# Head products of an mLSTM block in f16 halves with pairs summed on VectorE, and the next sequence's statistics moved behind the last chunk's heads

## Chip, cores and metric

One NeuronCore of a Trainium2 chip runs the whole program; the other cores are idle. The metric is the device time of one execution in microseconds. The kernel before took 1876.2 us, the median of 3 runs (1874.89 to 1881.56).

## The reference

Sixteen sequences of 512 tokens with 512 features pass through one block: layer norm, an mLSTM attention with 8 heads (query and key width 32, value width 64), a per-head norm, an output gate and a projection, all added to x; then layer norm and a feed-forward part of 2048 units whose weights are made ternary.

```python
def step(carry, xs):                       # over the 512 tokens of a sequence
    f_log = jax.nn.log_sigmoid(f_t)
    m_new = jnp.maximum(f_log + m, i_t)
    F = jnp.exp(f_log + m - m_new)
    I = jnp.exp(i_t - m_new)
    C_new = F[..., None, None] * C + (I[..., None] * k_t)[..., :, None] * v_t[..., None, :]
    n_new = F[..., None] * n + I[..., None] * k_t
    qs = q_t * scale
    h_num = jnp.einsum('bhd,bhdv->bhv', qs, C_new)
    qn = jnp.einsum('bhd,bhd->bh', qs, n_new)
    denom = jnp.maximum(jnp.abs(qn), jnp.exp(-m_new)) + EPS
    h = h_num / denom[..., None]
...
h_norm = _multihead_norm(h, gamma)         # (h - mean) * rsqrt(var + EPS) * gamma, per head
y = (jax.nn.sigmoid(o_preact) * h_norm) @ Wout.T
x = x + y                                  # layer norm of x goes in
x = x + gelu(layernorm(x) @ w1_q.T + b1) @ w2_q.T + b2
```

## The kernel before

The recurrence is computed in its chunked form. A sequence is four chunks `j` (or token tiles `t`) of 128 tokens. For each head the scores of a chunk (keys by queries, from f16 halves) are multiplied with a decay factor into the tile `dec` (f32, keys on the partitions) and masked; `vaug` holds the values of a tile with a column of ones appended, 8 heads x 65 columns. The product of `dec` and `vaug` gives numerator and normaliser of a head, and the state of the earlier chunks (`cst`) is added by a second product with the weighted queries `qw`.

Every engine's program is written out by hand, in order, and the engines meet by semaphores alone. The order of TensorE is that of `sequence(b, fb, ahead)`: the attention of sequence `b` interleaved with the feed-forward part of sequence `fb = b - 1`. In its order: `gates` (L1567), values (`tokens`, `late_values`), keys and queries (`features`), output gate; `up` of 16 feed-forward tiles (`hidden`), with the scores between them; then `down` in sixteen quarters. Four of these quarters carry a head chunk: `chunk(j, t, q)` calls `down` with `j`, and after each of its 8 matmuls comes one `chunk_head` (L1684), an f32 product of 128x128 weights (`dec`) and 65 columns (`vaug`) into one of the four banks of `psh`; the profile shows it as two records. At the end of a sequence `project` (L1692) multiplies the transposed, gated heads (`hoT`) with the output weights, tile by tile, with quarters of `down` between the first three of them; projections 2 and 3 follow each other, then come the gates and the values of the next sequence. Sequence 0 has no feed-forward part beside it; there the heads stand alone, and the weights of the feed-forward part are prepared between them. Behind the last attention there is only the feed-forward part of sequence 15.

PSUM banks alternate: `pa` by the number of its use, so the gates take the bank that `residual` of tile 2 frees, and the values the bank that `residual` of tile 3 frees. `psh` is one set of banks for all four chunks: chunk j+1 waits for `ph_free`, which VectorE gives when it has read chunk j.

The chain of a chunk's heads, from `ph_fill` on: VectorE `head_stats` (L1248): denominators `den` and sums `hsum` from `psh`, centred heads `cent` (in `kT`) from `psh`, which frees it; ACT `squares` (L868); VectorE reduces these to `hvar`; POOL `head_norm` (L572): a power (L574) and a multiplication (L577); VectorE `gated` (L1284), which for chunk j stands inside `head_stats` of chunk j+1 and for chunk 3 by itself; ACT `gated_hi` (L872) and POOL `gated_lo` (L579) make f16 halves; SP issues the transposing DMA into `hoT` (L487).

VectorE's order behind the heads matters here: `head_stats` of a chunk, `result` (`done`, L1333) of a feed-forward tile, `next_stats` (the layer norm statistics of `x` of sequence b+2, which sits in `xin`, L1106), then `gated(b, 3)`, `residual` (L1293) of tiles 0 and 1, `norm_apply` (L1120) of sequence b+2, and `residual` of tiles 2 and 3 with the last `result` between them. POOL beside it adds the bias to the residual (`residual_bias`, L584) and computes 1/sqrt (`layer_norm`). ACT's `tokens_hi` of the next sequence waits for `norm_apply`.

## Time and profile before

| | |
|---|---|
| median of 3 runs | 1876.2 us |
| profiled execution | 1875.94 us, span 1874.2 us |
| TensorE matmul busy | 1811.6 us, 97% |
| TensorE weight load busy | 945.5 us, 50% |
| VectorE busy | 1178.1 us, 63% |
| ACT busy | 1034.3 us, 55% |
| POOL busy | 507.4 us, 27% |
| TensorE clock granted | 0.98 of 2.4 GHz over the span, full in the middle |

Read the busy times with care: matmuls overlap in the records, so a share of 97% means a stream without holes rather than 97% of the array's peak. The page's other two parts that matter are its chain of the work that ended last and its costliest groups. For the rest the timeline of one sequence is read, that of sequence 9 with the window from 987 to 1034 us; its pattern repeats in sequences 1 to 13. In a timeline a row is a start, a duration, and what ran; "x2" are two records that follow each other.

### The profile page before, as it was taken

What the parts mean: (1) busy time and instruction counts of PE and PEld (TensorE: products, weight loads), DVE (VectorE), ACT (ScalarE), POOL (GpSimd) and SP (SyncE); (2) the same over time, 40 slices, a digit from 0 to 9 for tenths busy, and PEclk for the clock granted to TensorE, in tenths of its full rate; (3) what the DMA queues carried; (4) which work ended last, traced back from release to release, by engine and by line L of the source; (5) the groups of instructions that cost most, each with busy time, mean ns of one, the idle gap of its engine ahead of it and who ended that gap; (6) DMA issues with size and microseconds to landing.
All of it is one profiled execution on the core that took longest, in us unless ns stands there. A gap on an engine that the chain in (4) does not pass through costs nothing.

```text
span 1874.2 us, 30222 instructions
## 1 busy us (share of the span) xinstructions
PE 1811.6 (97%) x11900; PEld 945.5 (50%) x11900; DVE 1178.1 (63%) x2259; ACT 1034.3 (55%) x1711; POOL 507.4 (27%) x394
## 2 busy tenths in 40 slices
PE   5769999999999999999999999999999999999989
PEld 3454554545455454545545454554545445454544
DVE  6686575665757566575765657576565756645542
ACT  5757647274563727456372745737274473736523
POOL 1342131412314141231413123141312214131220
PEclk8879999999999999999999999999999999999989
DMA  8434125240422515042251503225150332413010
GB/s 278 145 102 119 29 61 129 51 139 24 129 39 52 139 46 144 23 117 51 52 138 46 145 23 106 62 51 139 46 144 17 103 72 51 117 45 99 12 40 23
DMA packets 233517, 156.86 MB, mean 84 GB/s; under 512 B 195088, under 2 KB 199312, under 8 KB 228256
## 3 DMA queue, kind: packets, MB, share of 16 engines
q1 hardware_dynamic: 231792, 151.79, 30.8%
q10 hardware_dynamic: 1584, 3.15, 0.5%
q8 instruction: 94, 1.54, 0.3%
q14 instruction: 47, 0.39, 0.1%
HBM read 90.48 MB, written 17.24 MB: 57 GB/s over the span
## 4 chain that ended last, share of the span: by engine, by line
PE 92%; DVE 2%; ACT 1%; issue 1%; DMA 0%; POOL 0%; POOLq 0%; DVEq 0%; ACTq 0%
PE pf L1714 24%; PE pf L1728 24%; PE pa L1606 19%; PE pa L1582 8%; PE psh L1606 6%; PE psh L1687 5%; PE psh L1681 1%; PE psh L1665 1%; PE pa L1573 1%; PE psh L1647 1%; PE psh L1620 1%; ACT dec L842 0%; DVE x2T L1078 0%; DVE dec L1245 0%; DVE x2T L1090 0%
## 5 line engine op out<-in xcount | busy, mean ns | idle before, releaser
L1728 PE MATMUL pf<-w2T,gT 128*128 128x512 f16 x2048 | 535.8, 379 | 0.0
L1714 PE MATMUL pf<-x2T,w1T 128*128 128x512 f16 x2048 | 457.2, 381 | 0.8 <-DVE x2T L1322 0.6
L1330 DVE SCALAR_TENSOR_TENSOR gT<-g,wscale,gT 128x512 f16<-128x512 f32 x256 | 214.7, 839 | 287.2 <-ACT gT L865 287.2
L1728 PEld LDWEIGHTS pf<-w2T,gT 128*128 128x128 f16 x2048 | 223.9, 111 | 175.9
L1714 PEld LDWEIGHTS pf<-x2T,w1T 128*128 128x128 f16 x2048 | 194.1, 98 | 234.3 <-issue 2.5
L862 ACT ACTIVATE g<-pf,b1c 128x512 f32<-128x512 f32 x256 | 175.6, 686 | 100.9 <-PE pf L1714 88.5
L1606 PE MATMUL pa<-wT,xT 128*128 128x512 f16 x960 | 213.6, 380 | 1.0 <-ACT sig L801 0.9
L870 ACT ACTIVATE ktok<-kT 128x512 f32<-128x512 f32 x64 | 40.3, 630 | 315.0 <-DVE kT L1268 315.0
L1687 PEld LDWEIGHTS psh<-vaug,dec 128*128 128x128 f32 x1024 | 183.0, 193 | 15.4 <-DVE cst L1234 1.2
L865 ACT ACTIVATE gT<-g,wscale 128x512 f16<-128x512 f32 x256 | 184.8, 722 | 8.4
L574 POOL TENSOR_TENSOR hinv<-hvar,half 128x8 f32<-128x8 f32 x64 | 105.0, 1640 | 298.4 <-DVE hvar L1281 298.4
L1606 PE MATMUL pa<-wT,hoT 128*128 128x512 f16 x768 | 177.3, 385 | 3.8 <-DVE xT L1131 3.8
L1582 PE MATMUL pa<-xT,wT 128*128 128x512 f16 x768 | 171.4, 379 | 0.1
L1687 PE MATMUL psh<-vaug,dec 128*128 128x65 f32 x1024 | 168.9, 252 | 0.9 <-DVE cst L1234 0.9
L842 ACT ACTIVATE dec<-dec,gtok 128x128 f32<-128x128 f32 x512 | 154.2, 390 | 0.0
L561 POOL TENSOR_SCALAR_AFFINE_SELECT dec<-dec 128x1024 f32<-128x1024 f32 x64 | 76.8, 1201 | 280.4 <-DVE dec L1245 280.4
L1606 PEld LDWEIGHTS pa<-wT,xT 128*128 128x128 f16 x960 | 92.6, 98 | 114.0 <-issue 7.0
L570 POOL TENSOR_TENSOR qw<-qw,qT 128x768 f32<-128x768 f32 x16 | 56.6, 3537 | 335.1 <-ACT sig L801 175.1
L581 POOL TENSOR_TENSOR qT<-kT,qT 128x512 f16<-128x512 f32 x64 | 74.3, 1161 | 198.1 <-ACT qT L877 198.1
L1606 PE MATMUL psh<-wT,xT 128*128 128x512 f16 x576 | 126.9, 379 | 0.0
L1606 PEld LDWEIGHTS pa<-wT,hoT 128*128 128x128 f16 x768 | 75.7, 99 | 96.0 <-issue 8.0
L1582 PEld LDWEIGHTS pa<-xT,wT 128*128 128x128 f16 x768 | 74.4, 98 | 87.1 <-DVE wT L1053 0.4
(202 smaller groups left out, 2154.9 us busy)
## 6 DMA issues: line engine op xcount, KB each, us to landing
dec<-gate_r SPq DMA_DIRECT2D x32, 1024.0 KB, 6.5
xin<-L_attn_x SPq DMA_DIRECT2D x16, 1024.0 KB, 5.3
out<-x1b SPq DMA_DIRECT2D x64, 256.0 KB, 2.2
xres<-L_attn_x SPq DMA_DIRECT2D x16, 512.0 KB, 6.3
xres<-L_attn_x SPq DMA_DIRECT2D x32, 256.0 KB, 2.9
qw<-gate_w SPq DMA_DIRECT2D x128, 48.0 KB, 5.8
gT<-L_ffn_w SPq DMA_DIRECT2D x5, 1024.0 KB, 5.0
gT<-L_ffn_w ACTq DMA_DIRECT2D x3, 1024.0 KB, 6.3
```

Of the source, the lines that this page charges most:

```text
L561: nc.gpsimd.affine_select(out=rows_of, in_=rows_of, compare_op=ALU.is_ge, fill=0.0, base=0, pattern=[[0, 2 * T], [1, P]], channel_multipli ...
L574: nc.gpsimd.tensor_tensor(hinv[:, :], hvar[:, :], half[:, :], ALU.pow).then_inc(pool_a, 1)
L581: nc.gpsimd.tensor_tensor(head_parts[j % 2][:, LO, :], cent[j % 2], head_parts[j % 2][:, HI, :], ALU.subtract).then_inc(ho_lo[j], 1)
L842: last = nc.scalar.activation(dec[:, h, tok(j)], dec[:, h, tok(j)], ACT.Exp, bias=gtok[:, j, ROW_C, h:h + 1])
L862: nc.scalar.activation(g32[:, f % 2, :], pf[:, use % 2, :], ACT.Gelu, bias=b1c[:, f:f + 1], scale=1.0 / X_SCALE).then_inc(pf_free[use % 2], 1)
L865: nc.scalar.activation(gT[:, HI, f, :], g32[:, f % 2, :], ACT.Copy, scale=wscale[:, W_GELU:W_GELU + 1]).then_inc(g_hi, 1)
L1330: nc.vector.scalar_tensor_tensor(gT[:, LO, f, :], g32[:, f % 2, :], wscale[:, W_GELU:W_GELU + 1], gT[:, HI, f, :], ALU.mult, ALU.subtract) ...
L1582: last = nc.tensor.matmul(bank, wT[:, ws, k, col:col + P], xT[:, xs, :, k, :], start=(k == 0 and n == 0), stop=(k == KD - 1 and n == 2))
L1606: last = nc.tensor.matmul(bank, src[:, xs, k, :], wT[:, ws, k, col:col + D], start=(k == 0 and n == 0), stop=(k == KD - 1 and n == 2))
L1687: last = nc.tensor.matmul(psh[:, i, g * VA:(g + 1) * VA], dec[:, h, tok(j)], vaug[:, j, h, :], start=(j == 0 and g == 0), stop=(g == HG - ...
L1714: last = nc.tensor.matmul(bank, w1T[:, k, tok(f)], x2T[:, part, :, k, :], start=(k == 0 and part == HI), stop=(k == KD - 1 and part == LO))
L1728: last = nc.tensor.matmul(bank, gT[:, part, f, tok(t)], w2T[:, f, :], start=(f == 0 and part == HI), stop=(f == NF - 1 and part == LO), sk ...
```

## The change

In all sequences but number 0 a head product becomes two f16 products. The decay tile and the values are each split in a high and a low half (high: the value rounded to f16; low: the rest), the two value halves of a head lie side by side (130 columns), and both decay halves are multiplied with this pair. PSUM then holds two columns for each result, and VectorE adds them in one reduction over the pair (`head_sum`, in SBUF), which also frees `psh`. In sequence 0 the product stays f32 and VectorE copies the result to `head_sum`. Scales are moved so that the halves fit in f16.

The splits are new operations: high halves of the values by POOL (`value_hi`, 4), low halves by VectorE (`value_lo`, 4); high halves of the decay by ACT (`decay_hi`, 4), low halves by VectorE for chunks 0 and 1 and by POOL for 2 and 3 (`decay_lo`). The high and low halves of chunk j overwrite the f32 decay of chunk j-1, those of chunk 0 lie in `qT`. So each `decay_hi` waits for the `decay_lo` before it. The value halves share their memory with `hoT` and with the halves of keys and queries.

The statistics of the next x (`next_stats`) no longer stand between the chunks' `head_stats`: tiles 0 and 1 come behind the last `head_stats`, tiles 2 and 3 behind `residual` of tile 0. In sequence 0 all four come there.

```diff
+        shared = sb("shared", [P, T * NH * 2 * VA], F16)
+        hoT = shared[:, 0:T * 2 * D].rearrange("p (t a k c) -> p t a k c", t=T, a=2, k=KD)
+        vparts = shared[:, :].rearrange("p (t n w) -> p t n w", t=T, n=NH)
...
-        by_bank = psh[:, :, 0:HG * VA].rearrange("p h (a v) -> p a h v", v=VA)
-        heads, norms = by_bank[:, :, :, 0:DHV], by_bank[:, :, :, DHV]
+        by_bank = psh[:, :, 0:HG * 2 * VA].rearrange("p h (a w v) -> p a h v w", a=HG, w=2)
+        sum_by_group = head_sum.rearrange("p (a h) v -> p a h v", a=HG)
+        heads, norms = sum_by_group[:, :, :, 0:DHV], sum_by_group[:, :, :, DHV]
...
+            def value_hi(b, t):
+                pool.wait_ge(pa_fill, pa_filled(b, score_use(NH - 1)))
+                nc.gpsimd.tensor_copy(vparts[:, t, :, 0:VA], vaug[:, t, :, :]).then_inc(vhi_ok, 1)
+
+            def decay_lo(b, j):
+                pool.wait_ge(dec_hi_ok, at(b - 1, T, j + 1))
+                nc.gpsimd.tensor_tensor(dec_parts(j)[:, :, LO, :], dec[:, :, tok(j)], dec_parts(j)[:, :, HI, :],
+                                        ALU.subtract).then_inc(dec_lo_ok[j], 1)
...
                     earlier_only(b, n)
+                    if n in (1, 2) and not first:
+                        value_hi(b, 2 * n - 2)
+                        value_hi(b, 2 * n - 1)
+                if not first:
+                    decay_lo(b, 2)
                 head_norm(b, 0)
+                if not first:
+                    decay_lo(b, 3)
...
+            def decay_hi(b, j):
+                if j == 0:
+                    act.wait_ge(masked, at(b, NH // 2, NH // 2))
+                    act.wait_ge(qw_ok, at(b, 1, 1))
+                    act.wait_ge(kq_split, at(b, 2, 2))
+                else:
+                    act.wait_ge(dec_lo_ok[j - 1], at(b - 1, 1, 1))
+                nc.scalar.activation(dec_parts(j)[:, :, HI, :], dec[:, :, tok(j)], ACT.Copy).then_inc(dec_hi_ok, 1)
...
-                    for f in range(NF):
+                    for f in range(NF - 3):
                         gelu(fb, f)
+                    decay_hi(b, 0)
+                    for f in range(NF - 3, NF):
+                        gelu(fb, f)
+                    decay_hi(b, 1)
...
+                if run_f:
+                    decay_hi(b, 2)
                 squares(b, 0)
                 if run_f:
                     sigmoids(b)
+                    decay_hi(b, 3)
...
+            def value_lo(b, t):
+                dve.wait_ge(vhi_ok, at(b - 1, T, t + 1))
+                nc.vector.tensor_tensor(vparts[:, t, :, VA:2 * VA], vaug[:, t, :, :], vparts[:, t, :, 0:VA],
+                                        ALU.subtract).then_inc(vlo_ok, 1)
...
-                nc.vector.tensor_tensor(den_of, norms, gtok[:, j, ROW_EM, :].rearrange("p (a h) -> p a h", h=H4), ALU.max)
+                if isinstance(b, int) and b == 0:
+                    nc.vector.tensor_copy(sum_by_group, by_bank[:, :, :, :, 0]).then_inc(ph_free, 1)
+                else:
+                    nc.vector.tensor_reduce(sum_by_group, by_bank, AX.X, ALU.add).then_inc(ph_free, 1)
+                dve.wait_ge(ph_free, at(b, PH_USES, U_H + j + 1))
+                nc.vector.scalar_tensor_tensor(den_of, gtok[:, j, ROW_EM, :].rearrange("p (a h) -> p a h", h=H4),
+                                               head_scale[:, 0:1], norms, ALU.mult, ALU.max)
...
                 state(b, 1)
-                hidden(10, 11, 12)
-                between(0)
-                state(b, 2)
-                hidden(13, 14, 15)
+                for t in range(T):
+                    if run_f:
+                        value_lo(b, t)
+                    hidden(10 + t)
+                    if t == 2:
+                        between(0)
+                        state(b, 2)
+                if run_f:
+                    decay_lo(b, 0)
+                    hidden(14, 15)
+                    decay_lo(b, 1)
...
                 head_stats(b, 0, ca)
                 done(0)
-                if run_f:
-                    next_stats(0)
...
                 done(2)
-                next_stats(*(range(3, T) if run_f else range(T)))
+                if run_f:
+                    next_stats(0, 1)
                 gated(b, 3)
                 between(4)
                 between(5)
                 residual(b, 0, ca)
+                next_stats(*(range(2, T) if run_f else range(T)))
...
             def chunk_head(b, j, h):
...
+                    parts = dec_parts(j)
+                    nc.tensor.matmul(psh[:, i, 2 * g * VA:2 * (g + 1) * VA], parts[:, h, HI, :], vparts[:, j, h, :],
+                                     start=(j == 0 and g == 0), stop=False, skip_group_check=True)
+                    last = nc.tensor.matmul(psh[:, i, 2 * g * VA:2 * (g + 1) * VA], parts[:, h, LO, :], vparts[:, j, h, :],
+                                            start=False, stop=(g == HG - 1), skip_group_check=True)
```

## Rows read from the trace of the kernel before

**Rows 1.** The page: the chain that ended last, by engine.

```profile
PE 92%; DVE 2%; ACT 1%; issue 1%; DMA 0%; POOL 0%; POOLq 0%; DVEq 0%; ACTq 0%
```

**Rows 2.** Timeline of TensorE, sequence 9 (start us, duration us, engine, line, what).

```profile
989.37 0.38 PE L1728 MATMUL pf<-w2T,gT 128*128 128x512 f16 x1
...
991.67 3.62 PE L1728 MATMUL pf<-w2T,gT 128*128 128x512 f16 x16
...
1023.75 3.62 PE L1728 MATMUL pf<-w2T,gT 128*128 128x512 f16 x16
1027.20 5.34 PE L1606 MATMUL pa<-wT,hoT 128*128 128x512 f16 x24
1032.47 1.49 PE L1573 MATMUL pa<-xT,wgT 128*64 128x512 f16 x12
1033.89 2.76 PE L1606 MATMUL pa<-wT,xT 128*128 128x512 f16 x12
```

**Rows 3.** Timeline of VectorE (DVE), the same sequence.

```profile
991.94 0.17 DVE L1259 TENSOR_TENSOR den<-psh,gtok 128x8 f32<-128x8 f32 x1 [2.64 <-PE psh L1687]
...
1013.68 0.17 DVE L1259 TENSOR_TENSOR den<-psh,gtok 128x8 f32<-128x8 f32 x1 [2.39 <-PE psh L1687]
1013.77 0.68 DVE L1260 TENSOR_REDUCE hsum<-psh 128x8 f32<-128x512 f32 x1
...
1017.08 0.17 DVE L1281 SCALAR_TENSOR_TENSOR hvar<-hsum,den 128x8 f32<-128x8 f32 x1
...
1021.10 0.69 DVE L1290 SCALAR_TENSOR_TENSOR kT<-kT,sig 128x512 f32<-128x512 f32 x1 [1.68 <-POOL kT L577]
1021.70 0.75 DVE L1300 SCALAR_TENSOR_TENSOR xres<-pa,evac,xres 128x512 f32<-128x512 f32 x1
1022.49 0.69 DVE L1303 BATCH_NORM_STATS2 stats<-xres 128x6 f32<-128x512 f32 x1
...
1025.99 2.78 DVE L1123 TENSOR_SCALAR xin<-xin,mean,rstd 128x512 f32<-128x512 f32 x4 [0.49 <-POOL rstd L541]
...
1032.58 0.75 DVE L1300 SCALAR_TENSOR_TENSOR xres<-pa,evac,xres 128x512 f32<-128x512 f32 x1 [0.32 <-PE pa L1606]
```

**Rows 4.** Timeline of ACT: the cast of the last gelu.

```profile
987.79 0.72 ACT L865 ACTIVATE gT<-g,wscale 128x512 f16<-128x512 f32 x1
```

**Rows 5.** DMA issues of the sequence (median us from issue to landing).

```profile
hoT<-qT SPq DMA_TRANSPOSE x4, 3.2
```

**Rows 6.** Timeline of TensorE, sequence 0: first and last of twelve in a row.

```profile
112.97 0.22 PE L1526 MATMUL pf<-ident,x2T 128*128 128x128 f16 x1
...
113.58 0.22 PE L1528 MATMUL pf<-ident,x2T 128*128 128x128 f16 x1
```

**Rows 7.** Groups by line, shapes apart (busy us, mean ns of one).

```profile
L1143 DVE SCALAR_TENSOR_TENSOR gT<-xres,gT 128x1024 f16<-128x1024 f32 x30 | 36.5, 1215 | 4.3 <-ACT gT L741 4.3
...
L741 ACT ACTIVATE gT<-xres 128x1024 f16<-128x1024 f32 x30 | 31.6, 1052 | 0.4
...
L1714 PEld LDWEIGHTS pf<-x2T,w1T 128*128 128x128 f16 x2048 | 194.1, 98 | 234.3 <-issue 2.5 <-DVE x2T L1322 1.0 <-ACT g L862 0.7
```

**Rows 8.** Timeline of POOL, sequence 9, chunk 3.

```profile
1018.31 1.63 POOL L574 TENSOR_TENSOR hinv<-hvar,half 128x8 f32<-128x8 f32 x1
...
1022.53 1.16 POOL L581 TENSOR_TENSOR qT<-kT,qT 128x512 f16<-128x512 f32 x1 [1.46 <-ACT qT L877]
1023.64 1.27 POOL L590 TENSOR_TENSOR x1b<-xres,b2r 128x512 f32<-128x512 f32 x1
```

**Rows 9.** Timelines of POOL and VectorE, sequence 0, where both work.

```profile
113.64 1.04 POOL L577 TENSOR_TENSOR kT<-kT,hinv 128x512 f32<-128x512 f32 x1
...
114.04 0.17 DVE L1263 SCALAR_TENSOR_TENSOR den<-psh,den 128x8 f32<-128x8 f32 x1
114.12 0.58 DVE L1264 TENSOR_SCALAR hsum<-hsum 128x8 f32<-128x8 f32 x1
```

**Rows 10.** Timeline of TensorE, sequence 0: a wait for the weight preparation.

```profile
147.95 0.27 PE L1526 MATMUL pf<-ident,x2T 128*128 128x128 f16 x1 [2.16 <-DVE x2T L1092]
```

More of the change, by code:

```diff
@@ L38 @@
 TOP = 2.0 ** 15
+V_SPLIT = 2.0 ** -5 / X_SCALE
+SCORE_SPLIT = 2.0 ** -16
 TINY = 2.0 ** -100
@@ L254, in block_program @@
         kq_split = sem("kq_split")
+        vhi_ok, vlo_ok = sem("vhi_ok"), sem("vlo_ok")
+        dec_hi_ok = sem("dec_hi_ok")
+        dec_lo_ok = [sem(f"dec_lo_ok{j}") for j in range(T)]
+        cent_ok = sem("cent_ok")
         sq_ok = sem("sq_ok")
@@ L1419, in sequence @@
                 done(1)
-                if run_f:
-                    next_stats(2)
                 weights_out(*USES_OUT[2:4])
@@ L1674, in chunk_state @@
                     pe.wait_ge(masked, at(b, NH // 2, NH // 2))
+                    if not (isinstance(b, int) and b == 0):
+                        pe.wait_ge(vlo_ok, at(b - 1, T, T))
+                if not (isinstance(b, int) and b == 0):
+                    pe.wait_ge(dec_lo_ok[j], at(b - 1, 1, 1))
                 if j == 1:
```

61 lines of the change are left out of this document (37 added, 24 removed).

## Prediction

> **What bounds the kernel now.** I read the page's chain of the work that ended last first [rows 1]: 92% of it is TensorE, so the end moves only by what TensorE's own stream gains, less the idle time that a late partner puts into it. Next comes TensorE's timeline in one middle sequence [rows 2]. The reader should see the pattern in a chunk: one matmul of `down` (128x512), then the two records of one f32 head product, then the next `down` matmul 0.38 us after the last. Then VectorE's timeline in the same sequence [rows 3], for when it comes to each head chunk and to each projection; then ACT, SP and POOL beside it [rows 4, 5, 8].
>
> **TensorE's part.** A pair of one `down` matmul and one head lasts 0.383 us (989.37 to 991.67 holds six), a `down` matmul alone 0.216 (1023.75 to 1027.20 holds sixteen) [rows 2]. So a head costs 0.383 - 0.216 = 0.167 us. The streamed columns don't change: f32 went twice over 65, f16 goes twice over 130. What changes are the weight loads. The nearest price of the new form is the run of twelve f16 128x128 matmuls, each with its own load: 0.61 us for eleven starts, 0.0555 us each at full clock [rows 6]. With 130 columns that is 0.0564, two are 0.113, and a head saves 0.054; since both f16 loads of a pair stand beside short matmuls I take 0.051. The bounds are a loss of 0.029 (each f16 product costs the 0.098 that its load lasts) [rows 7] and a gain of 0.054. Heads that change: 32 in each of 15 sequences, 480. **Gain: 480 x 0.051 = 24.5 us** (bounds -14 and 26), and a chunk's pitch falls from 7.25 (three pitches between 991.94 and 1013.68) [rows 3] to 6.84 us.
>
> The Trainium skill ("TensorE: Matmul & The Clock Gate", Back-to-back issue gap) gives about 81 ns for each matmul of 128 columns in a stream of loads and matmuls. By it the two would cost 0.162 and the gain would be 3 us. The trace's own run of such pairs disagrees [rows 6], and I go by the trace.
>
> **What is added elsewhere, up to chunk 0.** POOL gets four casts (128x520) behind the second and third mask; POOL is idle between masks and nobody waits before 988.8, so nothing. ACT gets four 128x1024 casts of 1.05 us, as L741 [rows 7]. The first stands ahead of gelu 13 of 16, where ACT has some 0.75 us spare, and delays it by about 0.3 us; TensorE needs that bank 0.9 us later. The second follows the last gelu. VectorE gets four `value_lo` of 128x520, 0.69 us, and two `decay_lo` of 1.21 us, as L1143 [rows 7]: 5.2 us in all. It idles about 1 us between two `gelu_lo` there, so this fits too; `decay_lo(0)` ends near 987.3 and TensorE wants it at 988.6. If that cover is gone, each us costs 15.
>
> **What is added to the head chain.** Let t = 0 be the moment when VectorE sees chunk 0 finished. After `gelu` 15 (its cast starts at 987.79) [rows 4] come decay_hi(1), decay_lo(1), decay_hi(2): 988.5 + 1.05 + 1.25 + 1.05 = 991.95, and t = 0 is 991.94 - 8 x 0.051 = 991.53. So POOL's `decay_lo(2)` starts at t = 0.5. Its price: POOL's f16 subtract of 512 elements takes 1.16 us, L581 [rows 8], so about 2.25 for 1024.
>
> `head_stats` grows: a reduce of 1040 elements from PSUM. That of 512 takes 0.68 [rows 3]; of this some 0.14 is fixed, as L1143 shows with 1024 in 1.21 [rows 7], and the rest goes by elements: 0.14 + 1040 / 512 x 0.54 = 1.23. The low bound is a second 0.68 (output is only 520), the high one 2.3 (if a reduction over pairs goes at half rate). From its start to `hvar` it took 3.40 us (1013.68 to 1017.08) and will take 4.66.
>
> And its small operations change place. `norms` and `heads` were in PSUM and are now in SBUF beside another SBUF operand. What that means the trace shows where POOL works at the same time: L1263, which reads PSUM, took its 0.17 us at 114.04 in the middle of POOL's L577, and L1264 behind it, which works within SBUF and takes 0.16 as a rule, took 0.58 and ended with it, 114.70 against 114.68 [rows 9]. So an operation of VectorE within SBUF that comes second waits for POOL's to end, and I take the same for the new forms of `den` and `cent`, and for POOL behind VectorE.
>
> The Trainium skill ("SBUF — State Buffer", Who interferes with whom) says it as an exclusive lock that a VectorE instruction with two SBUF inputs contends for, and one with a single SBUF input outside the two-port modes does not. It speaks against this change, which turns PSUM inputs into SBUF ones; were the lock only for L1264's kind, rival 1 would be the outcome.
>
> Walked through, in t:
> - Stats 0: reduce to 1.3, then `den` is held by POOL's decay_lo(2) to 2.75; hvar 6.6, result(0) to 7.3. It starts chunk 1 at 7.3, not 6.84.
> - POOL: pow 1.63 and multiply 1.04 [rows 8, 9] to 9.6, then decay_lo(3) (ACT has its high half about then, behind the sigmoid) from 9.7 to 12.0. Stats 1 stand still for it: `cent` at 12.2 to 12.5, hvar at 14.3, chunk 2 begun at 14.4 where 13.7 was possible.
> - Stats 2 end at 20.0, result(1) 20.7; stats 3 begin at 20.7 (possible: 20.5), lose 1 us to POOL's multiply of chunk 2, hvar 26.3. POOL's gated_lo(2), pow and multiply follow: gated(3) starts at g = 30.4 (30.4 to 30.85 by who comes first at 8.6). Before, it was 1021.10 - 991.94 = 29.16 [rows 3], with TensorE 1.24 us slower. Without the two POOL holds I get g = 29.2.
>
> **Behind the heads, where it is due.** TensorE ends the second-last projection (12 matmuls from 1027.20) 16.1 us after chunk 3's heads, starts the gates at 18.8 and the values at 20.2 (1013.68 against 1029.8, 1032.47, 1033.89) [rows 2, 3], which is now t = 36.6, 39.3, 40.7. It needs bank 0 from residual(2) at 39.3 and bank 1 from residual(3) at 40.7. VectorE's queue between: gated 0.61, residual 0.78, bn_stats 0.69, the moved next_stats(2,3), like bn_stats, 1.32, and mean_var, seven small operations, some 0.85, held 0.5 by POOL's residual_bias(0), L590, 1.27 us [rows 8]; residual(1) 0.78, bn_stats 0.69; norm_apply, which waits for POOL's rstd and residual_bias(1) and then takes 1.65 (1025.99, 2.78 with the wait for L590 in it) [rows 3]; then residual(2), bn_stats, result(3), residual(3): 2.9. That is g + 11.55: residual(3) is done at 41.95, not 40.7. In the profile before it is done at 1033.33 against 1033.89, 0.5 us ahead [rows 2, 3]. **Stall: 1.3 us per sequence** (0.1 with g = 29.2, 1.7 with 30.85), in the 13 sequences that still have a next x to normalise (1 to 13): -16.9 us. The transposed heads of chunk 3 leave when POOL ends, 33.0, with 0.4 for a transfer issued ahead, and land 3.2 later [rows 5], t = 36.6, just when wanted; before they had 2.5 us to spare (POOL began its last part at 1022.53) [rows 8].
>
> **Sequence 0** keeps f32 products and is bound by VectorE (TensorE waits 2.16 us for L1092) [rows 10]. It gets four PSUM copies of 520, 0.69 us each, 2.8 us, of which 0.6 goes into gaps: -2.2 us. The moved statistics stand ahead of the same work, so they give nothing.
>
> **Sum:** 24.5 - 16.9 - 2.2 = 5.4 us. The profiled execution took 1875.9 (span 1874.2 and 1.7 around it), 0.3 below the median of 1876.2. 1875.9 - 5.4 = 1870.5; I say **1870**. An error of 0.6 us in the walk either way is 8 us; the case itself covers 1862 to 1880.
>
> **Rivals.**
> 1. The lateness is absorbed. POOL's two subtractions fall into gaps of the chain, g stays at 29.2 and the stall at 0.1. For it: 0.5 us of carry at chunk 1 has to survive two pitches of 6.84 with 5.2 to 5.9 us of work. Against it: both holds are long (2.25) and the second sits in the middle of stats 1. 1875.9 - 24.5 + 1.3 + 2.2 = **1855**.
> 2. Slower: the pair reduction. If it runs at half rate (2.3 us), each `head_stats` takes 6.3 us with its result, against a pitch of 6.84, and any hold spills into the next chunk. g rises by three times about 0.8 to 32.8, residual(3) ends 3.7 us late: 13 x 3.7 = 48 against 24.5 and -2.2: **1902**. It turns to a loss as soon as the stall is over 1.7 us, g = 30.85, which is a reduce of only 1.4 us with the holds as walked. For it: no row reduces pairs. Against it: every f32 row of VectorE goes by its input count.
> 3. The loads bind and heads gain nothing: the old price stays, or each f16 product comes to the 0.098 us that its load lasts, as in L1714 [rows 7], 0.029 over now, 14 us; with the old pitch the stall is gone: 1875.9 + 2.2 + 0 to 14 = **1878 to 1892**. The run of twelve speaks against it [rows 6]. The skill's 81 ns would give this rival's low end.
>
> **How the numbers follow.** Forecast 0.50, rival 1 0.28, rival 2 0.14, rival 3 0.08. 0.5% (9.4 us) is about what a measurement of this kernel can tell from no change. The forecast's range reaches past 1866.8, a quarter of it, and past 1885.6 hardly: faster 0.28 + 0.13 = 0.41; same 0.35 + 0.04 = 0.39; slower 0.02 + 0.14 + 0.04 = 0.20. The range for 8 in 10 takes in rival 1 and the mild part of rival 2: 1852 to 1890.
>
> **What would show it.** Heads: a pair at 0.329 to 0.334 us instead of 0.383. Holds: den or cent operations of 1 us and more that end with a POOL instruction. Stall: TensorE idle before the gates or the values (L1573, L1606), released by L1300, 0.5 to 1.7 us in sequences 1 to 13 and none in 14. A middle sequence is shorter by 0.3 us in the forecast, by 1.5 in rival 1. The forecast is wrong if the values start without a wait, or if the reduce isn't between 1.1 and 1.4 us.

## The result and the profile after

The changed kernel takes **1883.2 us** (median of 20 runs, 1879.8 to 1886.3) where the kernel before takes 1876.1 in the same job (1874.0 to 1881.8). The ratio is 1.003, 95% interval 1.0021 to 1.0039: slower by 0.3%, where a gain, 1870, was forecast. 1883.2 lies within the range that was given, 1852 to 1890, but on the other side of the kernel before. The profiled execution took 1881.85, its span is 1880.1 (before: 1875.9 and 1874.2).

The chain of the work that ended last, from the page, is no longer TensorE alone [rows 1]; and two lines of the view of what TensorE waited for (us in total, times, longest) are new:

```profile
PE 60%; DVE 24%; POOL 5%; issue 4%; ACT 3%; DMA 0%; DVEq 0%; POOLq 0%; SPq 0%
```

```profile
PE pa L1680 <- DMA shared<-qT: 18.5, 15, 1.6
...
PE pa L1680 <- DVE xres L1371: 6.0, 12, 0.6
```

`shared<-qT` is the transfer that transposes a chunk's gated heads into `hoT`, and L1680 is the matmul line of the projections and values (L1606 before). Once in each of 15 sequences TensorE stands before the last projection until chunk 3's transposes land, and in 12 it stands a second time for residual(3).

TensorE's timeline in the stretch that the prediction calls sequence 9 shows the gain and the loss beside each other. (Counted from 0, as the table below counts, these are the heads and projections of sequence 8; the gates at their end are those of sequence 9.)

```profile
1002.62 0.38 PE L1813 MATMUL pf<-w2T,gT 128*128 128x512 f16 x1
1002.83 0.22 PE L1770 MATMUL psh<-shared,dec 128*128 128x130 f16 x1
1002.89 0.22 PE L1772 MATMUL psh<-shared,dec 128*128 128x130 f16 x1
...
1004.59 0.38 PE L1813 MATMUL pf<-w2T,gT 128*128 128x512 f16 x1
...
1032.33 2.75 PE L1680 MATMUL pa<-wT,shared 128*128 128x512 f16 x12
1036.34 2.77 PE L1680 MATMUL pa<-wT,shared 128*128 128x512 f16 x12 [1.25 <-DMA shared<-qT]
1039.03 1.49 PE L1647 MATMUL pa<-xT,wgT 128*64 128x512 f16 x12
1041.02 1.25 PE L1680 MATMUL pa<-wT,xT 128*128 128x512 f16 x5 [0.51 <-DVE xres L1371]
```

From 1002.62 to 1004.59 lie six pairs of `down` matmul and head, 0.328 us each instead of 0.383 [rows 2]. The next-but-last projection starts at 1032.33 and should be followed 2.59 us later, at 1034.92 (that is the step from 1026.28 to 1028.87 for the same 12 matmuls); the last one starts at 1036.34, 1.4 us late, and the values lose 0.5 more.

VectorE's timeline of that sequence. `t` is counted, as in the prediction, from 998.39, when it sees chunk 0 done:

```profile
998.39 1.24 DVE L1327 TENSOR_REDUCE ktok<-psh 128x520 f32<-128x1040 f32 x1 [0.78 <-PE psh L1772]
999.67 1.27 DVE L1329 SCALAR_TENSOR_TENSOR den<-gtok,head_scale,ktok 128x8 f32<-128x8 f32 x1
...
1005.19 1.24 DVE L1327 TENSOR_REDUCE ktok<-psh 128x520 f32<-128x1040 f32 x1
...
1007.95 1.92 DVE L1334 SCALAR_TENSOR_TENSOR den<-ktok,den 128x8 f32<-128x8 f32 x1
...
1013.79 1.24 DVE L1327 TENSOR_REDUCE ktok<-psh 128x520 f32<-128x1040 f32 x1 [1.19 <-POOL qT L607]
...
1020.38 1.24 DVE L1327 TENSOR_REDUCE ktok<-psh 128x520 f32<-128x1040 f32 x1 [0.52 <-POOL qT L607]
...
1029.61 0.69 DVE L1361 SCALAR_TENSOR_TENSOR kT<-kT,sig 128x512 f32<-128x512 f32 x1 [1.63 <-POOL kT L603]
...
1040.22 0.74 DVE L1371 SCALAR_TENSOR_TENSOR xres<-pa,evac,xres 128x512 f32<-128x512 f32 x1
```

and GpSimd's, POOL, beside it:

```profile
998.78 2.13 POOL L595 TENSOR_TENSOR dec<-dec 128x1024 f16<-128x1024 f32 x1 [14.55 <-ACT dec L913]
...
1007.72 2.13 POOL L595 TENSOR_TENSOR dec<-dec 128x1024 f16<-128x1024 f32 x1 [0.42 <-ACT dec L913]
1012.55 1.16 POOL L607 TENSOR_TENSOR qT<-kT,qT 128x512 f16<-128x512 f32 x1 [2.70 <-ACT qT L920]
```

The reader should see two kinds of lateness. Two operations of 8 columns, which take 0.23 and 0.17 us where GpSimd is idle, take 1.27 and 1.92 us, because POOL's `decay_lo(2)` and `decay_lo(3)` (L595) run at that time; the first ends with it (1000.94 and 1000.91), the second too (1009.87 and 1009.85). And the reductions of chunks 2 and 3 start late for another reason: `[1.19 <-POOL qT L607]`, the end of `gated_lo(0)` (1012.55 + 1.16 = 1013.71). That is the wait for `ho_lo[j - 2]` at the top of `head_stats`: the centred heads of chunk j lie where those of chunk j-2 lay, so they may be written only when GpSimd has made the low half of the latter. So gated(3), the gating of the last chunk's heads, starts at g = 1029.61 - 998.39 = 31.22 us; it was 29.16 before [rows 3].

By whole sequences (starts of the gates, before L1573, after L1647): from the second gates to the sixteenth the kernel before takes 14 x 109.95 us, the changed one 14 x 110.01. The second gates come at 159.04 instead of 152.89, and after the sixteenth it takes 180.95 us instead of 182.03. So 6.15 + 0.83 - 1.08 = 5.9, the whole difference of the spans.

### The profile page after: what moved, and what is told of

It is laid out like the page before. It is cut to its first block, busy times and chain, and to the rows that moved or that the text cites. A ratio compares the mean times of both kernels' runs of the same rounds, so it can differ in the third digit from the quotient of the medians.

```text
span 1880.1 us, 30591 instructions
## 1 busy us (share of the span) xinstructions
PE 1791.2 (95%) x11900; PEld 877.1 (47%) x11900; DVE 1397.0 (74%) x2415; ACT 1085.0 (58%) x1771; POOL 619.9 (33%) x484
## 4 chain that ended last, share of the span: by engine, by line
PE 60%; DVE 24%; POOL 5%; issue 4%; ACT 3%; DMA 0%; DVEq 0%; POOLq 0%; SPq 0%
PE pf L1799 24%; PE pa L1680 11%; PE pa L1656 8%; PE psh L1680 6%; PE pf L1813 6%; DVE ktok L1327 4%; POOL qT L607 3%; DVE den L1334 2%; DVE xres L1371 2%; DVE den L1329 2%; DVE hsum L1331 2%; DVE xin L1178 2%; DVE kT L1361 2%; DVE stats L1374 2%; ACT qT L920 1%
## 5 line engine op out<-in xcount | busy, mean ns | idle before, releaser
L1813 PE MATMUL pf<-w2T,gT 128*128 128x512 f16 x2048 | 511.8, 379 | 0.0
L1401 DVE SCALAR_TENSOR_TENSOR gT<-g,wscale,gT 128x512 f16<-128x512 f32 x256 | 236.2, 923 | 226.9 <-ACT gT L898 225.0
L1813 PEld LDWEIGHTS pf<-w2T,gT 128*128 128x128 f16 x2048 | 197.4, 98 | 176.0
L1680 PE MATMUL pa<-wT,xT 128*128 128x512 f16 x960 | 213.2, 380 | 7.1 <-DVE xres L1371 6.0
L1680 PE MATMUL pa<-wT,shared 128*128 128x512 f16 x768 | 179.3, 384 | 21.4 <-DMA shared<-qT 18.5
L1680 PEld LDWEIGHTS pa<-wT,xT 128*128 128x128 f16 x960 | 92.5, 98 | 120.6 <-DVE xres L1371 12.3
L595 POOL TENSOR_TENSOR dec<-dec 128x1024 f16<-128x1024 f32 x30 | 63.8, 2126 | 224.6 <-ACT dec L913 224.6
L1680 PEld LDWEIGHTS pa<-wT,shared 128*128 128x128 f16 x768 | 74.4, 99 | 117.1 <-DMA shared<-qT 25.9
L1680 PE MATMUL psh<-wT,xT 128*128 128x512 f16 x576 | 126.9, 379 | 0.0
L600 POOL TENSOR_TENSOR hinv<-hvar,half 128x8 f32<-128x8 f32 x64 | 105.0, 1641 | 64.8 <-DVE hvar L1352 64.8
L607 POOL TENSOR_TENSOR qT<-kT,qT 128x512 f16<-128x512 f32 x64 | 74.3, 1161 | 157.0 <-ACT qT L920 157.0
L616 POOL TENSOR_TENSOR x1b<-xres,b2r 128x512 f32<-128x512 f32 x64 | 81.1, 1269 | 81.5 <-DVE xres L1371 44.2
```

What stands on the lines that cost most here:

```text
L600: nc.gpsimd.tensor_tensor(hinv[:, :], hvar[:, :], half[:, :], ALU.pow).then_inc(pool_a, 1)
L607: nc.gpsimd.tensor_tensor(head_parts[j % 2][:, LO, :], cent[j % 2], head_parts[j % 2][:, HI, :], ALU.subtract).then_inc(ho_lo[j], 1)
L616: nc.gpsimd.tensor_tensor(x1b[:, t, :], xres[:, t, :], b2r[:, :], ALU.add).then_inc(x1b_ok, 1)
L1401: nc.vector.scalar_tensor_tensor(gT[:, LO, f, :], g32[:, f % 2, :], wscale[:, W_GELU:W_GELU + 1], gT[:, HI, f, :], ALU.mult, ALU.subtract) ...
L1680: last = nc.tensor.matmul(bank, src[:, xs, k, :], wT[:, ws, k, col:col + D], start=(k == 0 and n == 0), stop=(k == KD - 1 and n == 2))
L1813: last = nc.tensor.matmul(bank, gT[:, part, f, tok(t)], w2T[:, f, :], start=(f == 0 and part == HI), stop=(f == NF - 1 and part == LO), sk ...
```

## Experiments

All numbers of a row are from one profile of that kernel, the median and the ratio from its timed runs; the ratio is to the kernel before as it was timed in the same job (its median was 1874.7 to 1879.0 from job to job), so ratios compare better across rows than medians. "Middle" is the mean length of sequences 1 to 14 by the starts of the gates, g the time to gated(3) as above (median over the sequences), "2nd gates" their start in us.

| kernel | g | middle | 2nd gates | median us | ratio to before (95%) |
|---|---|---|---|---|---|
| before | 29.16 | 109.95 | 152.89 | 1876.1 | 1 |
| after | 31.22 | 110.01 | 159.04 | 1883.2 | 1.003 (1.0021 to 1.0039) |
| wait_at_cent | 30.48 | 109.30 | 159.16 | 1871.8 | 0.9965 (0.9953 to 0.9976) |
| pool_sliver | 29.64 | 108.52 | 161.53 | 1861.2 | 0.9906 (0.989 to 0.9921) |
| lows_on_vector | 30.12 | 108.92 | 159.00 | 1866.8 | 0.9944 (0.9925 to 0.9963) |
| hoT_first | 31.22 | 109.96 | 160.76 | 1880.8 | 1.0026 (1.0015 to 1.0036) |
| residual3_first | 31.21 | 110.50 | 159.85 | 1892.4 | 1.0079 (1.0058 to 1.01) |
| part2_only | 29.16 | 109.95 | 157.95 | 1877.4 | 0.9998 (0.9987 to 1.001) |
| stats_back | 31.22 | 110.06 | 156.01 | 1879.0 | 1.0012 (0.9998 to 1.0026) |
| seq0_as_before | 31.22 | 110.21 | 154.37 | 1880.7 | 1.0011 (0.9998 to 1.0024) |
| before_again | 29.16 | 109.95 | 156.38 | 1879.3 | one run |
| best2 | 29.77 | 108.59 | 151.84 | 1856.6 | 0.9891 (0.9861 to 0.9922) |
| best3 | 29.76 | 109.12 | 158.17 | 1866.0 | 0.9942 (0.9926 to 0.9958) |
| best4 | 30.01 | 108.12 | 151.18 | 1853.4 | 0.9874 (0.9853 to 0.9894) |

**Theory and rivals.** The theory after the result: gated(3) is late by two things, the holds by POOL that the prediction had and the wait for `ho_lo[j - 2]` that it had not; all that hangs behind gated(3) is then late by the same, and sequence 0 loses more than its copies. Three rivals: POOL's chain alone sets the pace (then moving the wait is worth nothing); the order of the transfers makes the transposes late, and with them the projection; or it is VectorE's queue behind gated(3) that counts.

### The wait that was missed

```diff
-                if j >= 2:
-                    dve.wait_ge(ho_lo[j - 2], at(b, 1, 1))
                 dve.wait_ge(ph_fill, at(b, PH_USES, U_H + j + 1))
...
+                if j >= 2:
+                    dve.wait_ge(ho_lo[j - 2], at(b, 1, 1))
                 nc.vector.tensor_tensor(by_head(cent[j % 2]), heads, per_head(hsum[:, :], DHV),
```

> The changed kernel with one wait moved: VectorE's wait for the low halves of the gated heads of two chunks before stands ahead of the subtraction that overwrites them, and no longer ahead of the reduction and the denominators. Theory (this wait, which my sum left out, holds each of the last two chunk statistics, 1.19 and 0.52 us in sequence 9): gated(3) starts some 1.0 to 1.7 us sooner than 31.2 us after VectorE sees chunk 0 done, the projection's wait for chunk 3's hoT falls from 1.25 us to under 0.4, the wait for residual(3) to under 0.2, and the sequences lose 1.1 to 1.7 us each: 1858 to 1868 us. Rival (GpSimd's own chain through inverse and gated low half sets the pace, and the wait only shows it): g stays within 0.3 us and the time within 3 us of the changed kernel's 1883. Rival (the two holds by GpSimd's decay_lo set it): the same, no gain from the wait.

Measured: g 30.48, a gain of 0.74, and 1871.8 us, 11 less than after. The two idle times are gone from VectorE's timeline, but a part came back inside small operations, which now fall on other work of POOL (inverse, L600, and so on):

```profile
1011.06 1.01 DVE L1340 SCALAR_TENSOR_TENSOR den<-den,head_scale 128x8 f32<-128x8 f32 x1
...
1016.44 1.04 DVE L1332 TENSOR_SCALAR hsum<-hsum 128x8 f32<-128x8 f32 x1
```

So 1.71 us of waiting were worth 0.74 in g. The wait for residual(3) falls from 6.0 to 0.8 us in all, that for the transposes from 18.5 to 13.2. The wait is a cause, and the rivals that gave it no worth are out; both my size for g (1.0 to 1.7) and the time (1858 to 1868) were too good. The rest of the 2.06 us by which g had risen is still there, 1.32, so the wait isn't the only cause.

### The holds by GpSimd

```diff
-                nc.gpsimd.tensor_tensor(dec_parts(j)[:, :, LO, :], dec[:, :, tok(j)], dec_parts(j)[:, :, HI, :],
+                nc.gpsimd.tensor_tensor(dec_parts(j)[:, 0:1, LO, :], dec[:, 0:1, tok(j)], dec_parts(j)[:, 0:1, HI, :],
...
-                    last = nc.tensor.matmul(psh[:, i, 2 * g * VA:2 * (g + 1) * VA], parts[:, h, LO, :], vparts[:, j, h, :],
+                    last = nc.tensor.matmul(psh[:, i, 2 * g * VA:2 * (g + 1) * VA], parts[:, h, LO if j < 2 else HI, :], vparts[:, j, h, :],
```

> The changed kernel, but GpSimd's decay_lo of chunks 2 and 3 works on one head instead of eight, and the low product of these two chunks takes the high half again as its stationary operand; so the low halves of the decays of chunks 2 and 3 are left out of the result. TensorE does the same number of products. Theory of the prediction (VectorE is held by the two operations of 2.13 us): the denominators of chunk 0 fall from 1.27 to 0.23 us and the one held 1.92 us to 0.5 or less, VectorE comes 1.5 to 2.5 us sooner to gated(3), the projection's waits vanish, and the time falls by 14 x 1.3 to 14 x 1.8 us, to 1858 to 1865. Rival (the wait for the low halves two chunks before takes it all back): that wait grows by what the holds gave and the time stays above 1875. Rival (GpSimd's place in the queue, not the hold): not told apart from the first here, since both go.

Measured: g 29.64 and 1861.2 us. Chunk 0's denominators fall to 0.23 us, and VectorE now waits for TensorE, 1.10 us ahead of chunk 1 and 1.78 ahead of chunk 2, as it did before the change (there 1.99 and 3.09):

```profile
991.21 0.23 DVE L1329 SCALAR_TENSOR_TENSOR den<-gtok,head_scale,ktok 128x8 f32<-128x8 f32 x1
...
1003.55 1.24 DVE L1327 TENSOR_REDUCE ktok<-psh 128x520 f32<-128x1040 f32 x1 [1.78 <-PE psh L1772]
```

The time is in the range that was expected (1858 to 1865). The wait for `ho_lo` vanished at chunk 2 with the holds, so there it bites only when something else has made the chain late; at chunk 3 0.53 us of it stayed with no hold at all. The next kernel gives nothing up: VectorE takes over both subtractions.

```diff
-                if not first:
-                    decay_lo(b, 2)
                 head_norm(b, 0)
-                if not first:
-                    decay_lo(b, 3)
...
+                late_lows = j == 0 and not (isinstance(b, int) and b == 0)
+                if late_lows:
+                    decay_lo(b, 2)
                 nc.vector.scalar_tensor_tensor(den_of, gtok[:, j, ROW_EM, :]...
...
+                if late_lows:
+                    decay_lo(b, 3)
                 dve.wait_ge(sq_ok, at(b, T, j + 1))
```

> The changed kernel, but VectorE itself makes the low halves of the decays of chunks 2 and 3, in places where it waited in the run with the sliver: chunk 2's behind the reduction of chunk 0's heads, chunk 3's where it waits for the squares of chunk 0; ScalarE makes the high half of chunk 3 ahead of those squares. Nothing is left out. Theory (the two operations of 2.13 us on GpSimd cost VectorE 1.0 + 2.4 us of holds, and VectorE had 1.1 and 1.8 us of slack ahead of the statistics of chunks 1 and 2 once they were gone): VectorE pays 2 x 1.22 us, statistics of chunk 2 start on TensorE's time (13.6 us after chunk 0 is seen done), gated(3) near 29.7 us, and the time is that of the run with the sliver, 1861 us, within 3. Rival (the work counts on VectorE wherever it stands): 2.4 us more per sequence than the sliver, g at 31 or later, 1880 or more.

Measured: g 30.12, 1866.8 us, where about 29.7 and 1861 within 3 were expected: better than the changed kernel, short of the sliver. VectorE does 2 x 1.23 us more than in the changed kernel and is 1.1 us earlier at gated(3): what an operation on GpSimd costs VectorE can be more than the operation itself on VectorE. The 0.5 us that it misses against the sliver stand in its timeline as the missed wait again (1.19 and 0.52 us ahead of chunks 2 and 3, as in after). I had expected chunk 2 on TensorE's time here, and left that wait in the kernel.

### The transfer, and the queue behind gated(3)

```diff
-                    if j == T - 1:
-                        residual(b, RES_TILES[2])
...
                                  transpose=True).then_inc(hoT_loaded[j], 16)
+                residual(b, RES_TILES[2])
```

> The changed kernel, but the sync engine issues the transposing transfer of chunk 3's gated heads ahead of the load of x's last tile, in all sequences. The load took 0.38 us of issue ahead of it, and in the run with the moved wait the fourth transposes landed 4.2 us after issue where the first three took 3.2 or so. Theory (my step that hoT(3) lands 3.2 us after issue was short by the load's share of the queues): the wait of projection 3 falls from 1.25 us in sequence 9 by 0.4 to 1.3 us, the wait for residual(3) behind it grows by up to 0.3 because VectorE's queue comes next, and the time falls by 14 x 0.4 to 14 x 0.9, to 1871 to 1878. Rival (VectorE's queue ahead of residual(3) binds right behind): the DMA's wait is only exchanged for one on residual(3), time within 2 us of 1883.

Measured: 1880.8 us, middle 109.96. TensorE's waits on the transposes halve (18.5 to 9.6 us in all), and that of the values on residual(3) grows (6.0 to 7.8):

```profile
PE pa L1679 <- DMA shared<-qT: 9.6, 15, 0.9
PE pa L1679 <- DVE xres L1370: 7.8, 13, 0.6
```

A new wait, of the gates on residual(2), makes 5.0 us in 12. So what was gained at the transposes came back, all but some 2 us, behind them, and the rival stands (ratio 1.0026 against 1.003). Transposes and residual(3) are about equally late, because both hang on g. The next edit puts residual(3) ahead of result(3) on top of this:

```diff
+                residual(b, 3, ca)
                 done(3)
-                residual(b, 3, ca)
```

> The changed kernel with the transposes of chunk 3's heads issued before the load of x's last tile (as in the run hoT_first), and VectorE's residual(3) ahead of result(3) instead of behind it. Theory (the wait of projection 3 was exchanged for one on residual(3), because VectorE's queue behind gated(3) is as late as the transposes): residual(3) runs 0.67 us sooner, the wait of the gates and values on it, 0.9 us in a sequence of hoT_first (0.41 and 0.4 to 0.6), goes, the one on the transposes, 0.68, stays; a sequence 109.96 - 0.67 = 109.3 us, and 1871 to 1874 us. Rival (it is residual(2) or GpSimd's queue that is late): the time stays at 1880.

Measured: **1892.4 us**, the worst of all, against 1871 to 1874 expected. The wait of the values for residual(3) is gone, as expected (that of the gates on residual(2), 5.1 us, is not), and this line is new:

```profile
PE psh L1687 <- ACT stack L811: 14.3, 14, 1.4
```

VectorE's gate chain itself starts no later: 3.57 us after the gates (1047.17 - 1043.60), as in `hoT_first` (1044.23 - 1040.66). But result(3) now comes 2.9 us after the gates' start instead of 0.6, since the statistics of residual(3) went ahead of it too, and its store later with it. GpSimd may overwrite `x1b` of tile 3 only when that store is done, so its residual_bias(3) (L615) moves into the gate chain. The view puts its wait down to ScalarE's L826, which ended 0.1 us before; but the store was issued at 1047.28, and the operation starts 2.14 us later, as in `hoT_first`, where the view names the store (issued at 1042.06, started at 1044.20):

```profile
1049.42 1.56 POOL L615 TENSOR_TENSOR x1b<-xres,b2r 128x512 f32<-128x512 f32 x1 [4.61 <-ACT vaug L826]
```

```profile
1049.78 1.48 DVE L1210 TENSOR_SCALAR sig<-qT 8x512 f32<-8x512 f32 x1
...
1052.19 1.00 DVE L1384 TENSOR_SCALAR xres<-xres,mean,rstd 128x512 f32<-128x512 f32 x2 [0.49 <-POOL rstd L619]
```

L1210 takes 0.41 us in `hoT_first`; here it is held by L615, which ends at 1050.98, and the next norm waits for GpSimd's inverse behind it. VectorE comes to the tile `stack` (L1233), which TensorE transposes next, 15.2 us after the gates instead of 13.65, and TensorE waits 1.0 us for it; in the profiles of before, after and `hoT_first` it never waits there. At the end of the program the wait for the last residual grows too, from 5.2 to 8.3 us. So slack in front of residual(3) was bought with slack that wasn't there behind it. The rival that I gave for `best3` had the place right (the head of the next sequence's gates), with too small a price and without the store as its link.

> The kernel of best2 (its four edits) with residual(3) ahead of result(3) too. Theory: the last wait of the middle sequences, 6.4 us in 13 (0.5 each, on residual(3)), goes, and nothing else comes up: a sequence 108.2 us, 1846 to 1852 in its better runs, 4 to 6 below best2. Rival: result(3), now last, holds VectorE's head of the next sequence's gates, and half of it comes back: 1850 to 1856.

Measured: 1866.0 us where 1846 to 1852 were expected, and 9 more than `best2`; the same line, 12.9 us in 14.

### The second edit, and sequence 0

> The kernel before with the second edit alone: statistics of the next x behind the last chunk's heads, in all sequences. Theory: the middle sequences keep their length (110.0 us; TensorE doesn't wait for VectorE there), sequence 0 ends 2 to 3.5 us later because its projection waits for what the statistics held up: 1878 to 1880 us. Rival (all of sequence 0's loss is the copies): within 1 us of the kernel before.

> The changed kernel without its second edit: the head products in halves, but the statistics of the next x at their old places, three tiles between the head statistics. Theory: in the middle sequences VectorE's chain to gated(3) is later by 3 x 0.64 us less what it waited for (1.19 and 0.52 us on GpSimd in sequence 9, which take up most of it), so g rises by 0.2 to 1 us, the moved work leaves the way of residual(3) by as much, and the sequences lengthen by 0.2 to 1 us; sequence 0 gains 1.8 to 2.5 us. Together 1882 to 1893. Rival (the move only feeds the delay in front of residual(3) and norm_apply): the time falls, to 1872 to 1880.

> The changed kernel, but sequence 0 as in the kernel before: its statistics read the heads in PSUM directly, without the copy, and the statistics of sequence 2's x stand ahead of gated(3) again (sequence 0 alone). Theory (sequence 0 lost 6.15 us by the start of the next gates, of which 2.8 are the four copies and the rest the moved statistics): the first gates start at 153 to 155 us instead of 159.0, and the time falls by 4 to 6 us, to 1877 to 1879. Rival (the lower clock of chunk 3's heads alone costs it): the start falls by under 2 us. The other sequences stay as they are.

> The kernel before, unchanged, to see how much the start of the second gates (152.9 us in the profile the prediction rests on) moves from run to run; its times lie at 1874 to 1875, 1879 and 1881.5. Theory (the clock in sequence 0 falls in different places, and the middle sequences are the same): a middle sequence 109.95 us again; second gates at 152.9, or 4 to 7 us later with the whole difference ahead of them. Rival: the scatter lies in the middle sequences.

The edits: `part2_only` is the kernel before with the moves of `next_stats` as the diff of the change has them, `stats_back` is after with each `next_stats` back at its old line. `seq0_as_before` is

```diff
+                direct = isinstance(b, int) and b == 0
+                heads, norms = by_bank[:, :, :, 0:DHV, 0], by_bank[:, :, :, DHV, 0]
+                if not direct:
+                    heads, norms = sum_by_group[:, :, :, 0:DHV], sum_by_group[:, :, :, DHV]
                     nc.vector.tensor_reduce(sum_by_group, by_bank, AX.X, ALU.add).then_inc(ph_free, 1)
...
-                if run_f:
-                    next_stats(0, 1)
+                next_stats(*(range(0, 2) if run_f else range(T)))
                 gated(b, 3)
```

In the middle sequences the second edit changes g by nothing: 31.22 with it and without it (`stats_back`), since the three statistics then stand where VectorE waits anyway (1.19 and 0.52 us ahead of chunks 2 and 3 in after, 0.59 and 0 here); I had expected 0.2 to 1 us more. What it does change is VectorE's queue behind gated(3): with it TensorE waits for residual(3), 6.0 us in 12 sequences, without it never. Twelve of the 14 middle sequences of `stats_back` take 109.2 to 110.0 us, 109.6 in the mean, against 110.0 in after; the other two take 112.7 and 112.9, because the transposes landed 5.5 and 5.7 us after their issue, against 3.6 in the sequence before the first of them. Why those two landed late no run shows. With them the time, 1879.0, lies in the range of the rival (1872 to 1880) and not in the theory's (1882 to 1893). Behind the long wait the projection ran slowly:

```profile
703.12 4.15 PE L1684 MATMUL pa<-wT,shared 128*128 128x512 f16 x12 [3.03 <-DMA shared<-qT]
```

In sequence 0 the moved statistics lengthen a wait. TensorE waits for the last weights (L1092 in [rows 10]) 4.01 us in each of the seven profiles of kernels that move them, and 2.16 or 2.17 in before, `stats_back`, `seq0_as_before` and `best4`: 1.85 us more. (In `before_again`, `best2` and `best3` the last wait at this place is 1.27 us and for ScalarE, behind an earlier one of 2.4 to 3.4.) Of `part2_only`:

```profile
152.24 0.27 PE L1522 MATMUL pf<-ident,x2T 128*128 128x128 f16 x1 [4.01 <-DVE x2T L1092]
```

Before, the statistics filled a gap in which VectorE waited for POOL ahead of gated(3) of sequence 0 (2.17 us in `part2_only`, where they are gone from it); moved behind residual(0) they stand in front of the weights. The times don't resolve this: the ratio of `part2_only` is 0.9998 (0.9987 to 1.001), which fits the rival, within 1 us of before, better than the theory's 2 to 3.5 us; the profiled execution, 1879.9 with the second gates 5 us late, is the slowest of its ten.

The copies are worth some 1.6 us if the two profiles that differ by them are set side by side (second gates at 156.01 in `stats_back`, 154.37 in `seq0_as_before`), but that is less than the second gates scatter: `before_again`, the same program as before, has them at 156.38, 3.5 us later, with all its middle sequences at 109.95. In the profile of before the granted clock of 120 to 130 us was 0.83 and chunk 3's heads (16 records) took 2.00 us; in `before_again` it was 0.50 and they took 3.67.

So of the 6.15 us of after, 1.85 are the statistics and some 1.6 the copies, and 2.7 are left. One program can differ by as much from run to run, but it need not be chance here: chunk 3's heads of sequence 0 take 3.67 us in all seven profiles with the copies, and in only two of the seven without them; and TensorE stands 4.87 us in after ahead of the transpositions before these heads, where it stood 2.90 in before. No run separates this from the scatter, so it stays open. By the ratios `seq0_as_before` (1.0011) gives back 3.6 us of after's 1.003, as much as the two known parts together, but the intervals of the two ratios touch. Its second gates came where they were expected (153 to 155 us), its time, 1880.7, above the 1877 to 1879 expected.

### All together

> The changed kernel with four edits: the wait for the low halves two chunks before only ahead of the subtraction; the low decays of chunks 2 and 3 on VectorE; the transposes of chunk 3's heads issued before the load of x's last tile; sequence 0 reading PSUM directly and with the statistics ahead of gated(3). Theory (each removes one cause of the lateness; with no stall left a sequence is 109.95 - 1.76 = 108.2 us): no wait of the projection in the middle sequences, 14 x 1.76 us gained on the kernel before and sequence 0 within 2 us of it: 1850 to 1856. Rival (the sliver's residue of 0.36 us waiting for residual(3) stays, since VectorE's work after gated(3) is the same): 1856 to 1862.

> The kernel of best2, with the statistics of the next x where VectorE waited in its trace: tile 0's ahead of chunk 2's heads (0.5 us of waiting there), tiles 1 to 3 with their mean and variance ahead of gated(3) (1.99 us of waiting behind two tiles), none behind residual(0). Theory (the 0.5 us that the values of the next sequence still wait for residual(3) is VectorE's queue behind gated(3), which gets 2.4 us shorter): the wait goes without touching what comes after residual(3), a sequence 108.2 us against 108.59, and 1847 to 1856 us, 4 to 6 below best2 at the same start. Rival (GpSimd's queue to the inverse for norm_apply, or the transposes, is next and as late): 108.4 to 108.7 us a sequence, within 2 us of best2. Rival (the statistics delay gated(3)): 109 us or more.

`best4` has the moved wait, the low decays on VectorE, the transposes first, sequence 0 as before, and the statistics in VectorE's gaps; against `best2` (the two statistics behind residual(0) are gone too):

```diff
                 head_stats(b, 1, ca)
+                if run_f:
+                    next_stats(0)
...
-                next_stats(*(range(0, 2) if run_f else range(T)))
+                next_stats(*(range(1, T) if run_f else range(T)))
                 gated(b, 3)
```

Measured: `best2` 1856.6 us, with one wait left, for residual(3) (6.4 us in 13), which is the rival that was given (1856 to 1862); `best4` **1853.4 us** (1846.1 to 1855.0), as expected (1847 to 1856), 1.3% below before and, by the medians of two jobs, 1.6% below after (1853.4 / 1883.2). Its TensorE timeline at the place where after had two waits:

```profile
1011.14 5.34 PE L1683 MATMUL pa<-wT,shared 128*128 128x512 f16 x24
1016.42 1.49 PE L1650 MATMUL pa<-xT,wgT 128*64 128x512 f16 x12
1017.84 2.76 PE L1683 MATMUL pa<-wT,xT 128*128 128x512 f16 x12
```

Thirteen of its 14 middle sequences take 108.07 or 108.08 us (in the other, 108.73, the transposes landed 4.5 us after their issue instead of 3.1). That is what TensorE's stream is worth without a stall: 109.95 - 108.07 = 1.88 us for 32 heads, and the changed kernel's stall is 110.01 - 108.07 = 1.94.

## Why the prediction was wrong

- **TensorE's part: right.** 0.383 - 0.328 = 0.055 us a head against 0.051, 26.3 us against 24.5. The stall-free sequence gives 1.88, 28.2 us for 15; 1.75 of it are the pairs, the other 0.13 I have no row for. Rival 3 is out. The 81 ns of the Trainium skill ("TensorE: Matmul & The Clock Gate", Back-to-back issue gap) would have left a gain of 3 us; the measured pair leaves 26.
- **The reduction: right.** 1.24 us against 1.23, 60 times. Rival 2's half rate is out.
- **The holds: right in kind.** The two POOL operations take 2.13 against 2.25, and hold VectorE until they end; the first starts at t = 0.39 where 0.5 was said (the sum for it gives 991.85, not 991.95); `cent` of stats 1 starts at t = 11.9 (12.2 to 12.5 said). `pool_sliver` shows that they are most of it.
- **Statistics of chunks 2 and 3: the step that failed.** The stall was the term mis-sized most, and this is why. The walk lets chunk 2 begin at 14.4, as soon as stats 1 and VectorE's queue allow. Measured: 15.4, and chunk 3 at 22.0 instead of 20.7. The wait for `ho_lo[j - 2]`, two lines above the one whose cost I worked out, was put at nothing. It never showed in the profile of before, where `gated_lo` ended 2.6 us ahead of it; the holds, the longer statistics and the shorter pitch made it count. g is 31.22, not 30.4. Part of it was given back in the last round (9.2 us where 9.7 was said). `wait_at_cent` is the kernel that the walk describes, without this wait: g is 30.48 (30.4 said), the stall 109.30 - 108.07 = 1.23 us (1.3 said), the time 1871.8 (1870 said). That the time agrees so well is in part luck, since a larger gain and a dearer sequence 0 cancel in it; and the stall has the size but not the place that was said: TensorE waits 13.2 us in all for the transposes, and 0.8 for residual(3). That g comes out is the walk's own merit, with this one wait missing.
- **Behind gated(3): right.** From gated(3) to the end of residual(3) 11.35 us against 11.55 (the terms named in the prediction add up to 10.8; the rest is `norm_apply`'s wait, which had no number there). So residual(3) is done at t = 42.6, and the values wanted it at 40.7: 1.9 us of stall, which is the 1.94 of the whole run, against 1.3. The turning point stood in rival 2: a loss from g = 30.85. It was passed, by another mechanism than the rival's.
- **The transposes: wrong by a little, and it counts.** "Just when wanted" was 36.6; they were used at 37.95. 0.8 of this is g, 0.5 the landing, 3.7 us where I took the median 3.2 of all four; the fourth goes out beside the load of x's last tile. It also brought the stall to sequences 14 and 15, for which I had said none: nothing of the next x is needed there, but the transposes are. As `hoT_first` shows, both waits cover nearly the same time, so this adds little outside those two.
- **Sequence 0: half.** The copies may cost about what I said, 1.6 against 2.2, by two single profiles. "The moved statistics stand ahead of the same work, so they give nothing" is wrong by 1.85 us. Another 2.7 us stay open.
- **The sum.** In the profiles: heads 15 x 1.88 = 28.2 gained; stalls 14 x 1.94 = 27.2 and about 1 us in sequence 15 lost; sequence 0 6.15 lost: about -6 where +5.4 was forecast, and the spans say -5.9 (the medians -7.1). The terms that were mis-sized are the stall (1.94 for 1.3 us, and in two more sequences: 11 us) and sequence 0 (4, of which 2.7 are without a shown cause), against 4 us more gain.

## What to carry to other kernels

Before moving work onto an engine's chain, list every wait on that chain, the ones that never show in the trace above all: each has a slack, and the profile of before tells how much. A rate gained on the bounding engine shortens the time of every partner; here 1.9 us a sequence were gained, and given back to two operations on the engine that VectorE has to wait for, and to a wait with no need to stand where it stood. And an operation that is put off takes along what waits for it: result(3) cost little where it stood, and 9 us behind residual(3) (`best3` against `best2`), by the store and the GpSimd operation that wait for it.

## What the runs showed of the chip that was not expected

- VectorE's operations of 8 columns in SBUF took up to 1.92 us beside a GpSimd operation of 2.13 (0.17 alone), while the reduction of 1040 elements out of PSUM took 1.24 with L595 at work beside it (998.39), as in all 60 cases (mean 1.242). The hold hit only the operation behind it. When the two long operations were taken from GpSimd, doing them on VectorE as well left VectorE 1.1 us earlier. The Trainium skill ("SBUF — State Buffer", Who interferes with whom) speaks of an exclusive lock between the two, for VectorE instructions with two SBUF inputs or in a two-port mode, and not for reductions; the rows of `den` and of the reduction agree. Operations with one SBUF input were held as well (L1332 1.04 us in `wait_at_cent`, L1210 1.48 in `residual3_first`); no row tells whether they ran in such a mode.
- A transposing transfer of the same size landed 3.1 us after its issue (the second of a sequence), 3.2 to 4.7 when the load of 256 KB went ahead of it (the fourth, in the profiles of before and after and of the experiments that keep this order), but 5.5 and 5.7 in two sequences of `stats_back`. When it went first it took 3.1 to 3.75 in `hoT_first`, and 3.0 to 3.1 in `best2` and `best4` but for one of 4.5.
- After an idle time of 2.6 us in the midst of the program (`seq0_as_before`, sequence 13) the mean granted clock of the next 5 us was 0.66, so part of them ran at 1.2 GHz, and twelve matmuls took 4.45 us instead of 2.75; after waits of 1.25 us, sequence by sequence, they kept 2.77 at full clock (1.00 from 1036 to 1041 us in after). In these rows the long stall costs 1.7 us more than itself:

```profile
1583.58 4.45 PE L1684 MATMUL pa<-wT,shared 128*128 128x512 f16 x12 [2.60 <-DMA shared<-qT]
...
1583.00:1588.00 5.00, 4.42 (x14) 1.48 (x16) 3.95 (x7) 1.91 (x1) 1.46 (x2) 0.66 0.02 9
```
(timeline of TensorE, and below it the view by stretches: busy us and counts of PE, PEld, DVE, ACT, POOL, then the granted clock, the DMA share and GB/s.)
